# A window-attention stage whose scores stand ahead of the tasks of the slot before

## What is computed

```python
y = _mhsa(_window_partition(x), w_qkv, b_qkv, w_o, b_o, None)
y = _window_reverse(y)
ys = jnp.roll(y, shift=(-SH, -SW), axis=(1, 2))
ys = _mhsa(_window_partition(ys), w_qkv, b_qkv, w_o, b_o, mask)
ys = _window_reverse(ys)
return jnp.roll(ys, shift=(SH, SW), axis=(1, 2))
...
# in _mhsa
scores = jnp.einsum('bqhd,bkhd->bhqk', q, k) / jnp.sqrt(jnp.float32(hd))
if mask is not None:
    scores = scores + mask[:, None, :, :]
attn = jax.nn.softmax(scores, axis=-1)
out = jnp.einsum('bhqk,bkhd->bqhd', attn, v).reshape(B, S, D)
...
x = x + _L0_conv_ref(_ln_c(x), ...)
t = t + _L0_ffn_ref(_ln_t(t), ..., L0_ffn_edge_index)
```

## Time and profile before

| | us |
|---|---|
| median of 3 runs | 7988.18 (7985.07 to 7991.1) |
| profiled execution, its own time | 7973.06 |
| its span | 7971.5 |
| VectorE busy over the span | 4950.7 (62%) |
| TensorE busy over the span | 3948.5 (50%) |
| GpSimd busy over the span | 4965.8 (62%) |
| ScalarE busy over the span | 2081.6 (26%) |

### The profile page before, as it was taken

How to read it: one execution, slowest core, us unless ns; L and a number is a source line. 1 busy time by engine, 2 the same in 40 slices (tenths; PEclk the granted TensorE clock), 3 DMA queues, 4 the chain that set the end, 5 groups by cost and what they waited for, 6 DMA issues and landing times. The chain is left out here.

```text
span 7971.5 us, 90293 instructions
## 1 busy us (share of the span) xinstructions
PE 3948.5 (50%) x32216; PEld 2508.5 (31%) x32216; DVE 4950.7 (62%) x6417; ACT 2081.6 (26%) x4057; POOL 4965.8 (62%) x5602
## 2 busy tenths in 40 slices
PE   5889999987433433433433433433433433433246
PEld 3666666664221221222222222212212212212112
DVE  9999999997544545545545545545545545545456
ACT  4777777775111111111111111111111111111000
POOL 4222222212777777777777777777777777777684
PEclk8999999997666666666666666666666666666578
DMA  1222222222111211211211211111111111111467
GB/s 50 56 59 60 58 61 58 60 56 69 38 33 32 44 33 32 44 32 32 44 32 32 44 32 34 42 32 37 39 32 37 39 32 38 38 32 36 130 182 223
DMA packets 503671, 417.67 MB, mean 52 GB/s; under 512 B 160546, under 2 KB 400338, under 8 KB 502866
## 3 DMA queue, kind: packets, MB, share of 16 engines
q1 hardware_dynamic: 355842, 356.89, 14.2%
q0 software_dynamic: 147552, 56.96, 7.4%
HBM read 203.44 MB, written 176.45 MB: 48 GB/s over the span
## 5 line engine op out<-in xcount | busy, mean ns | idle before, releaser
L1622 POOL DMA_INDIRECT edge_G<-node_rows,edge_src x4352 | 4129.2, 949 | 1326.3 <-issue 1326.3
L1677 PE MATMUL edge_hbank<-edge_xt,edge_w 128*128 128x512 f32 x1024 | 720.8, 861 | 2757.9 <-ACT edge_hid L1647 2741.9
L1426 DVE TENSOR_TENSOR edge_oh<-edge_wbank,edge_dlf 128x3072 bf16<-128x3072 f32 x512 | 1682.6, 3349 | 55.7 <-PE edge_cbank L1702 40.6
L1383 DVE COPY edge_O<-edge_O 128x24 f32<-128x24 f32 x64 | 12.5, 195 | 2354.0 <-DMA edge_G<-node_rows,edge_src 2354.0
L1677 PEld LDWEIGHTS edge_hbank<-edge_xt,edge_w 128*128 128x128 f32 x1024 | 253.2, 274 | 3189.7 <-ACT edge_hid L1647 3035.8
L1702 PE MATMUL edge_cbank<-edge_oh 128*128 128x256 bf16 x4096 | 805.9, 367 | 647.3 <-DVE edge_oh L1426 646.9
L1657 ACT ACTIVATE edge_w<-edge_w 128x272 f32<-128x272 f32 x64 | 27.5, 429 | 4053.0 <-DVE edge_w L1397 4053.0
L569 POOL TENSOR_TENSOR attn_nw<-attn_st 128x8 f32<-128x8 f32 x64 | 42.4, 662 | 1403.7 <-DVE attn_st L1024 1403.7
L1702 PEld LDWEIGHTS edge_cbank<-edge_oh 128*128 128x128 bf16 x4096 | 478.6, 125 | 951.0 <-DVE edge_oh L1426 814.8
L1035 DVE TENSOR_TENSOR attn_keys<-attn_keys 128x1024 f32<-128x1024 f32 (+1 forms) x340 | 477.0, 1403 | 8.7 <-DVE attn_keys L1040 0.5
L1040 DVE TENSOR_TENSOR attn_keys<-attn_keys 128x1024 f32<-128x1024 f32 (+1 forms) x340 | 475.6, 1399 | 0.1
(11 more groups left out here) (280 smaller groups left out, 6389.7 us busy)
## 6 DMA issues: line engine op xcount, KB each, us to landing
edge_G<-node_rows,edge_src POOLq DMA_INDIRECT x4352, 2.4
expert_out<-edge_yo SPq DMA_DIRECT2D x64, 1024.0 KB, 4.4
comb_ye<-expert_out SPq DMA_DIRECT2D x32, 2048.0 KB, 13.4
state_rows<-edge_O SPq DMA_DIRECT2D x64, 816.0 KB
attn_km<-attn_kT SPq DMA_DIRECT2D x1024, 32.0 KB, 2.0
attn_xin<-in_x SPq DMA_DIRECT2D x32, 512.0 KB, 4.4
attn_xres<-in_x SPq DMA_DIRECT2D x32, 512.0 KB, 5.4
x_rows<-attn_x SPq DMA_DIRECT2D x32, 512.0 KB, 3.4
```

The source lines that it names most:

```text
L1426: dve.tensor_tensor(oh[:, r:r + WIDE, :, :].rearrange("p t k n -> p (t k) n"), iota.unsqueeze(1).to_broadcast([P, 3 * WIDE, P]), dlf[:, t: ...
L1622: pool.indirect_dma_start(G[b][:, t, :], None, node_rows, bass.IndirectOffsetOnAxis(ap=src[b][:, t:t + 1], axis=0)).then_inc(s_g[b][2 * t ...
L1677: pe.matmul(hbank[k % 2][:, :], w1[:, k // HB, (k % HB) * P:(k % HB + 1) * P], xt[b][:, :], start=True, stop=True).then_inc(s_l1, 1)
```

## The change

In TensorE's program of the first stage the waiting and the scores of a slot become a function `slot_scores`. It is called for slot j + 1 after turn and weigh of slot j and ahead of the tasks of slot j. For slot 0 it is called where it stood, so behind the tasks of the slot 7 before. All other engines' programs are the same.

```diff
+            def slot_scores(n, j):
+                if not streams(n):
+                    return
+                if n * PAIRS + j > 0:
+                    pe.wait_ge(s_sub, n * PAIRS + j)
+                for s in streams(n):
+                    last = scores(n, s, j)
+                last.then_inc(s_sc, 1)
...
                 for j in range(PAIRS):
-                    if streams(n):
-                        if n * PAIRS + j > 0:
-                            pe.wait_ge(s_sub, n * PAIRS + j)
-                        for s in streams(n):
-                            last = scores(n, s, j)
-                        last.then_inc(s_sc, 1)
+                    if j == 0:
+                        slot_scores(n, 0)
                     k, i = later(n, j, 2)
                     if streams(k):
                         turn(k, i)
                     k, i = later(n, j, 3)
                     if streams(k):
                         weigh(k, i)
+                    if j + 1 < PAIRS:
+                        slot_scores(n, j + 1)
                     for task in tasks_of(n, j):
```

## The result

| | before | changed |
|---|---|---|
| median | 7986.62 us (4 runs, 7981.82 to 7991.1) | 8101.28 us (4 runs, 8099.46 to 8112.79) |
| profiled execution | 7973.06 us | 8112.79 us |
| TensorE busy | 3948.5 us | 3984.9 us |
| VectorE busy | 4950.7 us | 4955.5 us |
| VectorE waits for TensorE, first stage (reduction + reciprocal) | 83.4 + 0 us | 125.7 + 78.4 us |

The ratio is 1.0143 (95% interval 1.0131 to 1.0155): 115 us slower. The two profiled executions are 140 us apart, since the one of before lies under all of its kernel's timed runs and the one of the changed kernel is the slowest of its four.

What follows compares the result with a forecast made beforehand. VectorE bounds the early first stage; later VectorE and TensorE are both near their limit. Images' extra waits of 50, 11 and 22 us sum to 83 us, added to 7973.06 and shifted to the median: 8071 us, range 8014 to 8110.

Steps and rivals of the forecast that it cites:

- The bound and the place: First stage: VectorE 95% and TensorE 92% busy from 600 to 1550 us; VectorE's reduction waits mostly at slot 0.
- (a): Slots 1 to 7: scores can be ready about a task block earlier; put at 0, at most 83.4 us gained.
- (b): Image end: tasks(6) and tasks(7) between slot 7's and next slot 0's scores; 0.8 to 1.6 us later per image.
- the image walked: First-stage image ending at 1043.30 us, whose timeline gave a 13.62 us chain and 1.6 us later end.
- the 0.5 us at slot 1: TensorE idles 0.5 us before S(1), waiting for slot 0's subtraction; VectorE needs S(1) only a full slot later.
- (c): Even slots: VectorE's reciprocal waits for later weighted sums, 3.0 us mid-image; 0 where sort columns are absent or in slots 0, 1.
- The sum: First stage: 16 middle images 3.1 us each, eight early 1.4, nine others 2.5; together 83 us.
- rival 4: TensorE's clock: busy share falls from 92% to some 87%, as where the clock was 0.98; no drop expected, no chance given.
- Rival 3: Slot 4's scores held by late key copies: 2 to 3 us more per image, 60 us more, 8131 us; chance 0.06.
- the main case: Longer image ends with part of the late weighted sums' cost: 8014 to 8104 us, chance 0.80.
- The rule on gaps: Skill page: start dependencies ending the most-contended engine's gaps sooner; by it time would fall by up to 83.4 us.

Runs made afterwards that it cites:

- slot 7 alone: Kernel before with only slot 7's scores moved ahead of slot 6's tasks; 8061.47 us, ratio 1.0089.
- slot 4 alone: Kernel before with only slot 4's scores moved ahead of slot 3's tasks; 8065.07 us, ratio 1.0105.
- the late division: Changed kernel with VectorE's division of the weighted sums at the slot's end, behind its sort operations and statistics; 8086.1 us, ratio 1.0129.

## Why the prediction was right, and where its sizes were off

The forecast was 8071 us in a range of 8014 to 8110, slower with 0.85; measured were 8101 us.

- **The bound and the place.** Right. All but 9 of the 140 us between the profiled executions are in the first stage, and the wait stands at slot 0 of nearly every image.
- **(a), nothing to win in slots 1 to 7.** Their reductions did win 27 us of waiting (32.5 to 5.0). It was no gain for the kernel, as said, since an image ends when its longest chain does.
- **(b), the longer end.** The chain was right to 0.15 us in the image walked (13.47 us against 13.62). That it starts at slot 6's subtraction held in the kernel with slot 7 alone, where slot 7's scores started 0.1 us behind it in each of the 28 images. In the changed kernel they started 1.6 us behind it on average, and 3.2 us in the image walked, where 3.1 of them are the half clock. What I called a matter of the image's end is more general: slot 4 alone and slot 7 alone cost 82 and 72 us. Each single move puts two blocks of tasks between two scores at one place and none at another, and at the place with none TensorE waits for the subtraction, because there is one set of score banks: with slot 7 alone it idles 58 us ahead of slot 7's scores, where it idled 4. That idle time uses up its lead. In the changed kernel the 0.5 us at slot 1 that I put at no cost is the smaller piece, 21 us in all; ahead of slot 2's scores it idles 68 us, since the work of tasks(0) without sort columns is far shorter than a slot. The prediction has no term for that.
- **(c), the weighted sums.** The wait exists, 4.14 us where 3.0 was worked out. It stands also in early images without sort columns, where I had put it at 0. As an addition to (b) it was worth some 15 us, by the late division, if that difference is taken at its face.
- **The sum.** Per image, from the starts of slot 0 in VectorE's two timelines: the 16 middle images grew by 4.7 us each (3.1 forecast), the eight early ones by 4.0 (1.4 forecast), and all the others by 23 us together (22 forecast). So the mis-sized terms are the middle and above all the early images, and there the last two. The first stage grew by 131 us in the profiled pair and the median by 115, against 83.
- **A term at nothing, the clock (rival 4).** I took the granted clock from the busy share. The share came out as forecast, 87% from 600 to 1550 us, but the clock is 0.96 there and not 0.98, and from 150 to 600 us it fell from 0.98 to 0.92. The middle images that kept their clock grew by 2.1 us, less than my 3.1; the middle and early ones that lost it most grew by 7 to 10. So the two mechanisms of the sum were there, but the total fell into the range partly by luck: what they cost at full clock was taken too high in the middle, and what goes with the half clock, which was left out, made up for it and more. How much of the growth the clock caused stays open.
- **Rival 3, the keys.** Half right: slot 4's scores do wait for them (49.0 us), and the room ahead of the reduction covers that wait, but not the one of the reciprocal behind the weighing. Worth some 15 us, not 60, and it stood beside the main case, not in its place.
- **The rule on gaps.** By it the kernel would have got faster. It names the right gap; what the runs add is that the dependency which ends that gap has to be the one that starts sooner. With slot 0's scores moved it holds: 35 us for one line of order.

## What to carry to other kernels

When two engines hand one buffer back and forth and both are near their limit, moving one producer step past a block of other work makes a seam at which two blocks of work meet, wherever it is, and another place at which the producer idles. Moving every step takes the seam away, but was no cure here either (107 us), since the weighted sums and the keys then come late. Look first in which iteration the consumer waits, and move that one (35 us won). Putting the step into the middle of the block everywhere won 57 us, with fewer waits for the double-buffered banks beside it. And look whether the moved idle time costs the engine its clock.

## What the runs showed of the hardware that I had not expected

TensorE lost clock in short stretches inside a busy stage: in the image walked the granted clock fell to half at 1062.19 us, in a wait of 2.62 us, and the 16 score matmuls behind it took 1.98 us instead of 1.09; this is the lower of the two levels, 1.2 GHz for 2.4. In the same image it was at half again from 1096.32 to 1103.15 us, where TensorE had idled 1.27 us until 1093.96 and idled 0.22 us more within. From 150 to 1800 us the time at half clock went from 27 to 167 us. The mean score matmul went from 402 to 416 ns and TensorE's busy time by 36.4 us.
